# A LoRA and mixture-of-experts kernel on one core: the W stage opens with a quarter of all eight blocks, two sums to a PSUM bank, and six LoRA factors are issued behind it

## The chip, the cores and the metric

One core of one Trainium2 chip runs the whole kernel. The time is device microseconds of that core. The kernel before takes 283.78 us, the median of three runs (283.76 to 284.56). The names of the engines are those of the profile: PE is the matrix engine's products and PEld its weight loads, DVE is VectorE, ACT is ScalarE, POOL is GpSimd, SP is SyncE; SPq and ACTq are instructions that these two only issue, DMAs above all.

## The reference

```python
# x (8, 512, 2048); W (2048, 2048); b (2048); slot (8,) chooses LoRA factors for each batch
A, Bm = lora_As[slot], lora_Bs[slot]                      # (8, 2048, 16), (8, 16, 2048)
y = einsum('bti,oi->bto', x, W) + b + 2.0 * (x @ A) @ Bm  # conditioned layer
logits = einsum('bsd,ed->bse', y, route_w)                # 8 experts
weight = one_hot(argmax(logits)) * max(logits)
h = einsum('bsd,erd->bser', y, A_moe)                     # rank 16 of each expert
out = x + einsum('bser,eor->bso', weight[..., None] * h, Bw)
```

## The kernel before

y itself is never formed. Only 136 of its linear functions are used: the 128 rows of the experts' A and the 8 rows of route_w. They stand side by side as PT (2048 x 136). So the kernel first multiplies W with PT (the **W stage**), which gives a matrix M of 2048 x 136, and then multiplies x with M. All matrices are float32; M and x are split into a high and a low part (m_hi, m_lo, x_hi, x_lo), and three products of parts take the place of one.

**The W stage.** The inputs of W are cut into 8 blocks of 256 (`NWB`), its outputs into 4 quarters of 512 (`NWH`). A piece (block, part) is 512 KB, and 32 pieces go through a ring of 8 slots (`w_ring`). Four 128-row chunks times two halves of a block make 8 products of 136 columns, which the profile shows as 16 records. A block's two sums lie in the two banks of one PSUM tensor (`w_bank`), each in the first 136 of 512 columns, and are complete when all four parts were added. `ORDER` is the order of the pieces: all parts of blocks 0 to 3 (`OPEN` = 4) are taken part by part, and then blocks 4 to 7 each with its four parts. The first part of the opening is loaded in two halves (`load_open`, `w_open`): the head (W's first half piece and the PT rows that it needs, 392 KB) and half pieces of 256 KB. PT's other rows come behind the pieces that `PT_AFTER` names. SyncE issues all these loads, in order; from the ninth load on each waits until a piece is done (`t_w`).

After 20 pieces (`BP_AT`) the matrix engine computes the LoRA-B sums (L708, from `lb_cols`, which GpSimd rearranges) and the bias sum (L713). These go into `bank_l` and `bank_e[1]`, both in the tensor `bank_rl`.

**Taking the sums.** ScalarE copies a block's M out of PSUM: m_hi, and the 8 route columns into the two buffers of `ext` (`m_block`, L395). VectorE then forms m_lo = M - m_hi (`m_block`, L508) and counts it in `v_m`. The matrix engine waits for `v_m` where it begins a block whose PSUM tensor an earlier block used (`w_piece`). At `n == BP_AT // NWH`, 5, ScalarE takes the LoRA and bias sums (`bp`, `pb`), and issues eight DMAs from bp and one from pb into `g_a`, and then `load_a(2, NB)`: the A factors of batches 2 to 7, 128 KB each, into `la`. An engine's instructions and DMA issues are done in the order of its program.

**Behind the W stage.** For each batch `extension(b)` multiplies x with the 32 columns of `ext[b % 2]`: 8 route columns and the batch's 16 LoRA-A columns, which GpSimd copies there from `la` (`load_ext`, L367). The copy for batch 2 waits for all six factors of `load_a(2, NB)` (`d_la`). Then 8 steps of 6 products form h for the batch (L797, L811, L826). The order is: extension 0, steps of batch 0, extensions 1 and 2, steps of batch 1 with the output products of batch 0 between them, and so on. In the last step of batch 0, before the last product, the matrix engine waits for GpSimd's copy for batch 2:

```python
                        if b == 0 and j == NP2 - 1:
...
                                pe.wait_ge(g_ext, TWIN + 1)
```

ScalarE's `top(0)` (e_top, L455) follows extension 0. x comes in pieces of 1 MB through a ring of 12, issued by SyncE among and behind the last W loads; the outputs go back through the same ring.

## Time and profile before

| | us |
|---|---|
| median of three runs | 283.78 |
| span of the profiled execution, first to last instruction | 282.3 |
| PE busy | 276.7 |
| PEld busy | 220.0 |
| DVE busy | 200.5 |
| ACT busy | 110.2 |
| POOL busy | 15.0 |

The median lies 1.5 us over the profiled span; of the profiled execution the profile gives the span alone. The busy time is a share of the whole span and says which engine has no room. Where an engine waited, and for whom, stands in its timeline: the start of an instruction, its duration, and in brackets the idle time before it with the engine that ended it. Two views go by another clock: the landing of a DMA is counted from its issue, and the rows by slices of time are means.

### The profile page before, as it was taken

Reading aid. Unit: us, or ns where it says so; the run is one execution under the profiler, and the core shown is the slowest. Engines: PE = TensorE matmul, PEld = TensorE weight load, DVE = VectorE, ACT = ScalarE, POOL = GpSimd, SP = SyncE. Lnnn points to the kernel's source line nnn. Section 1 sums busy time; section 2 is a strip of 40 time slices with the busy share of each in tenths; the row PEclk is TensorE's granted clock in tenths of the full one; section 3 lists DMA queues with packets and bytes.
Section 4 is the critical chain, followed back from the end, with each engine's and each line's share of the span. In section 5 each row is a group of like instructions: output and inputs, shape, how many; then the busy total and the mean of one; then the engine's idle time right before and its main releaser. Section 6 shows DMA issues by size and latency. Waiting matters only on the chain.

```text
span 282.3 us, 4100 instructions
## 1 busy us (share of the span) xinstructions
PE 276.7 (98%) x1601; PEld 220.0 (78%) x1601; DVE 200.5 (71%) x223; ACT 110.2 (39%) x151; POOL 15.0 (5%) x46
## 2 busy tenths in 40 slices
PE   8999999999999999999999999999999999999993
PEld 5999999997773888888488758867885888588882
DVE  0053100077497889999889969996998799788794
ACT  0001201097684645534274346426533743370000
POOL 7600030000001000000000000000000000000000
PEclk9999999999999999999999999999999999999998
DMA  7999999999992034999966993999399859606688
GB/s 226 414 404 397 397 412 410 378 399 415 416 426 97 2 149 188 351 346 388 404 259 230 425 389 152 352 402 404 130 373 399 320 167 420 288 22 253 261 354 322
DMA packets 19014, 88.50 MB, mean 313 GB/s; under 512 B 2346, under 2 KB 4530, under 8 KB 11442
## 3 DMA queue, kind: packets, MB, share of 16 engines
q1 hardware_dynamic: 15696, 83.70, 75.7%
q10 hardware_dynamic: 3298, 4.54, 4.4%
q8 instruction: 12, 0.20, 0.3%
q14 instruction: 8, 0.07, 0.1%
HBM read 54.60 MB, written 33.55 MB: 312 GB/s over the span
## 4 chain that ended last, share of the span: by engine, by line
PE 90%; DVE 6%; DMA 2%; SPq 1%; issue 0%; DVEq 0%
PE bank_out L670 15%; PE bank_eh L797 11%; PE bank_eh L811 10%; PE bank_eh L826 10%; PE bank_out L736 9%; PE bank_out L759 9%; PE bank_out L750 9%; PE bank_rl L777 5%; PE bank_eh L777 5%; DVE x_ring L654 4%; PE bank_eh L670 2%; PE bank_rl L670 2%; DMA head_sb<-head 2%; PE bank_rl L708 1%; PE bank_eh L832 1%; PE bank_rl L831 1%
## 5 line engine op out<-in xcount | busy, mean ns | idle before, releaser
L393 ACT ACTIVATE x_hi<-x_ring 128x1024 fp32r<-128x1024 f32 x64 | 67.4, 1060 | 57.5 <-PE bank_eh L826 57.2
L506 DVE TENSOR_TENSOR x_lo<-x_ring,x_hi 128x1024 fp32r<-128x1024 f32 x64 | 77.5, 1220 | 8.6 <-ACT x_hi L393 8.6
L595 DVE TENSOR_TENSOR x_ring<-bank_out,x_ring 128x1024 f32<-128x1024 f32 x54 | 65.7, 1218 | 2.9 <-PE bank_out L759 2.8
L797 PE MATMUL bank_eh<-x_hi,m_hi 128*128 128x512 f32 x128 | 50.6, 395 | 0.0
L811 PE MATMUL bank_eh<-x_lo,m_hi 128*128 128x512 f32 x128 | 49.9, 390 | 0.0
L826 PE MATMUL bank_eh<-x_hi,m_lo 128*128 128x512 f32 x128 | 49.8, 389 | 0.0
L736 PE MATMUL bank_out<-wh_hi,bw_hi 128*128 128x512 f32 x120 | 46.7, 389 | 0.0
L750 PE MATMUL bank_out<-wh_lo,bw_hi 128*128 128x512 f32 x120 | 46.7, 389 | 0.0
L759 PE MATMUL bank_out<-wh_hi,bw_lo 128*128 128x512 f32 x120 | 46.7, 389 | 0.0
L670 PE MATMUL bank_out<-pt,w_ring 128*128 128x136 f32 x288 | 34.6, 279 | 0.0
L670 PEld LDWEIGHTS bank_out<-pt,w_ring 128*128 128x128 f32 x288 | 33.9, 190 | 0.2 <-DMA w_ring<-W 0.2
L797 PEld LDWEIGHTS bank_eh<-x_hi,m_hi 128*128 128x128 f32 x128 | 24.0, 188 | 10.7 <-issue 5.9
L826 PEld LDWEIGHTS bank_eh<-x_hi,m_lo 128*128 128x128 f32 x128 | 24.0, 188 | 5.1
L811 PEld LDWEIGHTS bank_eh<-x_lo,m_hi 128*128 128x128 f32 x128 | 24.0, 188 | 4.8
L759 PEld LDWEIGHTS bank_out<-wh_hi,bw_lo 128*128 128x128 f32 x120 | 22.5, 188 | 4.7
L750 PEld LDWEIGHTS bank_out<-wh_lo,bw_hi 128*128 128x128 f32 x120 | 22.5, 188 | 4.7
L736 PEld LDWEIGHTS bank_out<-wh_hi,bw_hi 128*128 128x128 f32 x120 | 22.5, 188 | 4.7
L777 PE MATMUL bank_rl<-x_ring,ext 128*32 128x512 f32 x128 | 14.6, 595 | 0.0
L777 PE MATMUL bank_eh<-x_ring,ext 128*32 128x512 f32 x128 | 14.5, 595 | 0.0
L393 ACT ACTIVATE wh_hi<-wh 128x512 fp32r<-128x512 f32 x8 | 5.1, 632 | 23.5 <-DVE wh L584 23.5
L506 DVE TENSOR_TENSOR m_lo<-bank_out,m_hi 128x256 fp32r<-128x256 f32 x6 | 2.5, 424 | 16.4 <-ACT ext L393 16.4
L506 DVE TENSOR_TENSOR bw_lo<-x_ring,bw_hi 128x2048 fp32r<-128x2048 f32 x1 | 2.3, 2291 | 14.5 <-ACT bw_hi L393 14.5
(99 smaller groups left out, 220.6 us busy)
## 6 DMA issues: line engine op xcount, KB each, us to landing
x_ring<-xT SPq DMA_DIRECT2D x32, 1024.0 KB, 8.0
outT<-x_ring SPq DMA_DIRECT2D x26, 1024.0 KB, 4.8
w_ring<-W SPq DMA_DIRECT2D x28, 512.0 KB, 10.8
outT<-x_ring SPq DMA_DIRECT2D x5, 512.0 KB, 2.8
outT<-x_ring ACTq DMA_DIRECT2D x4, 512.0 KB, 2.8
w_ring<-W SPq DMA_DIRECT2D x6, 256.0 KB, 5.3
outT<-x_ring SPq DMA_DIRECT2D x5, 256.0 KB, 2.7
x_ring<-loraB ACTq DMA_DIRECT2D x8, 128.0 KB, 9.8
```

The source lines that it names most:

```text
L393: act.activation(out, in_, ACT.Copy).then_inc(done, 1)
L506: dve.tensor_tensor(out, a, b, ALU.subtract).then_inc(done, 1)
L595: dve.tensor_tensor(x, out_bank(b, j)[:, :, :], x, ALU.add).then_inc(v_out, 1)
L654: dve.tensor_tensor(x, out_bank(NB - 1, c // 2)[:, c % 2, :], x, ALU.add).then_inc(v_out, 1)
L670: last = mm(bank, w_chunk(n, o, i), pt_chunk(k), start=(k == 0), stop=(k == C - 1))
L736: mm(out, bw_hi[:, o], hi, start=True, stop=False)
L750: mm(out, bw_hi[:, o], lo, start=False, stop=False)
L759: last = mm(out, bw_lo[:, o], hi, start=False, stop=True)
L777: last = mm(bank_e[b % 2][g * GROUP:(g + 1) * GROUP, :], ext[b % 2][:, c, :], x_pair(b, c // 2)[:, c % 2, :], start=(r == 0), stop=(r == C ...
L797: mm(bank_h, m_hi[:, c, :], hi, start=(c == 0), stop=False)
L811: mm(bank_h, m_hi[:, c, :], lo, start=False, stop=False)
L826: last = mm(bank_h, m_lo[:, c, :], hi, start=False, stop=(c == C - 1))
```

## The change

- `ORDER` begins with part 0 of all eight blocks, in two halves each; then come parts 1 to 3 of blocks 0 to 3, part by part, and then parts 1 to 3 of blocks 4, 5, 6 and 7. PT's later rows are issued behind loads 7, 10 and 13.
- Two blocks share a PSUM tensor: columns 0 to 135 of each bank for blocks 0 to 3, columns 136 to 271 for blocks 4 to 7 (block 4 with 2, 5 with 3, 6 with 0, 7 with 1). The LoRA-B sums and the bias sum take columns 272 to 407 of `bank_rl`, the tensor of blocks 3 and 5. Only the first product in a bank carries the start flag.
- The sums are taken in the order 0, 1, 3, 2, 4, 5, 6, 7 (`TAKEN`). The LoRA and bias sums, with their nine DMAs, are taken before block 3; block 2 is taken when block 4 is done.
- The matrix engine waits for `v_m` at one place of the W stage alone: part 1 of block 5, for the third m_lo.
- `load_a(2, NB)` stands behind the last block's copies.

```diff
--- before.py
+++ after.py
@@ -73,11 +73,16 @@
     HEAD_W = HO * WI
     PT_PARTS = [(4, 8), (8, 12), (12, 16)]
     NPT = len(PT_PARTS)
-    PT_AFTER = {3: 0, 6: 1, 9: 2}
+    PT_AFTER = {7: 0, 10: 1, 13: 2}
     OPEN = NWB // 2
-    ORDER = [(blk, part) for part in range(NWH) for blk in range(OPEN)] + [
-        (blk, part) for blk in range(OPEN, NWB) for part in range(NWH)]
+    ORDER = [(blk, 0) for blk in range(NWB)] + [
+        (blk, part) for part in range(1, NWH) for blk in range(OPEN)] + [
+        (blk, part) for blk in range(OPEN, NWB) for part in range(1, NWH)]
     DONE = [max(n for n in range(NWP) if ORDER[n][0] == blk) + 1 for blk in range(NWB)]
+
+
+    TAKEN = [0, 1, 3, 2, 4, 5, 6, 7]
+    READY = [DONE[OPEN] if blk == 2 else DONE[blk] for blk in range(NWB)]
     assert ER == P and WI == 2 * P and NWB == NP2 and NB * R == P and BIAS_ROW < GROUP
 
     ctx = ExitStack()
@@ -169,7 +174,7 @@
         d_slots, d_bias, d_bw, d_lb, d_la0, d_la = (sem(n) for n in ("d_slots", "d_bias", "d_bw", "d_lb", "d_la0", "d_la"))
         d_pt = [sem(f"d_pt{i}") for i in range(NPT)]
         d_head = [sem(f"d_head{h}") for h in range(NHEAD)]
-        d_w_half = [sem(f"d_w_half{n}") for n in range(1, OPEN)]
+        d_w_half = [sem(f"d_w_half{n}") for n in range(1, NWB)]
         d_w = [sem(f"d_w{i}") for i in range(WRING)]
         d_x = [sem(f"d_x{i}") for i in range(XRING)]
         d_out = [sem(f"d_out{i}") for i in range(XRING)]
@@ -232,7 +237,11 @@
 
         def w_bank(blk):
 
-            return (*bank_out, bank_eh, bank_rl)[blk] if blk < OPEN else bank_out[blk % 2]
+            bank = (*bank_out, bank_eh, bank_rl)[blk] if blk < OPEN else (bank_eh, bank_rl, *bank_out)[blk - OPEN]
+            at = PN * (blk // OPEN)
+            return bank[:, :, at:at + PN]
+
+        lora_sums, bias_sums = (bank_rl[:, i, 2 * PN:3 * PN] for i in (1, 0))
 
         def out_bank(b, j):
 
@@ -273,7 +282,7 @@
 
             def load_open(h):
                 sp.dma_start(head_sb[:, h, :], head[h]).then_inc(d_head[h], 16)
-                for n in range(1, OPEN):
+                for n in range(1, NWB):
                     blk, part = ORDER[n]
                     o = slice(h * HO, (h + 1) * HO)
                     sp.dma_start(w_ring[:, n, o, :], W[blk, part, :, o, :]).then_inc(d_w_half[n - 1] if h == 0 else d_w[n], 16)
@@ -294,8 +303,8 @@
 
             for h in range(NHEAD):
                 load_open(h)
-            for n in range(OPEN - 1, NWP):
-                if n >= OPEN:
+            for n in range(NWB - 1, NWP):
+                if n >= NWB:
                     load_w(n)
                 if n in PT_AFTER:
                     k = PT_AFTER[n]
@@ -394,8 +403,10 @@
 
             def m_block(n):
 
-                act.wait_ge(t_w, DONE[n])
-                sums = w_bank(n)[:, :, 0:PN]
+                act.wait_ge(t_w, READY[n])
+                if n == OPEN:
+                    act.wait_ge(v_m, OPEN)
+                sums = w_bank(n)
                 copy(m_hi[:, 2 * n:2 * n + 2, :], sums[:, :, E:PN], a_m)
                 for i in range(2):
                     copy(ext[i][:, 2 * n:2 * n + 2, 0:E], sums[:, :, 0:E], a_m)
@@ -410,26 +421,25 @@
                 copy(x_hi[:, g % SRING, :, :], x_pair(b, j), a_xhi)
 
             act.wait_ge(g_zero, ZEROED)
-            for n in range(NWB):
+            for n, blk in enumerate(TAKEN):
                 if n == 0:
                     act.wait_ge(t_w, LB_AT)
                     for b in range(NB):
                         act.dma_start(lb[:, b, :, :].rearrange("p c r -> p (c r)"),
                                       loraB[bass.ds(slot[b], 1), :, :].rearrange("s p n -> p (s n)")).then_inc(d_lb, 16)
                     load_a(0, 2)
-                if n == BP_AT // NWH:
+                if n == 2:
                     act.wait_ge(t_bp, 1)
-                    act.activation(bp[:, E:XN], bank_l[:, 0:PN], ACT.Copy, scale=float(SCALING)).then_inc(a_bp, 1)
-                    act.activation(bp[:, 0:E], bank_l[:, 0:E], ACT.Copy, scale=float(SCALING)).then_inc(a_bp, 1)
                     act.wait_ge(t_pb, 1)
-                    copy(pb[:, E:XN], bank_e[1][0:1, 0:PN], a_bp)
-                    copy(pb[:, 0:E], bank_e[1][0:1, 0:E], a_bp)
+                    act.activation(bp[:, E:XN], lora_sums, ACT.Copy, scale=float(SCALING)).then_inc(a_bp, 1)
+                    act.activation(bp[:, 0:E], lora_sums[:, 0:E], ACT.Copy, scale=float(SCALING)).then_inc(a_bp, 1)
+                    copy(pb[:, E:XN], bias_sums[0:1, :], a_bp)
+                    copy(pb[:, 0:E], bias_sums[0:1, 0:E], a_bp)
                     act.wait_ge(a_bp, 4)
                     act.wait_ge(g_const, 4)
                     for b in range(NB):
                         act.dma_start(g_a[E:E + R, b, :], bp[b * R:(b + 1) * R, :]).then_inc(d_g, 16)
                     act.dma_start(g_a[BIAS_ROW:BIAS_ROW + 1, :, :], pb[:, :].unsqueeze(1).broadcast_to([1, NB, XN])).then_inc(d_g, 16)
-                    load_a(2, NB)
                 if n == NWB - 2:
                     act.wait_ge(d_g, 16 * (NB + 1))
                     for part, form in G_PARTS:
@@ -446,7 +456,8 @@
                 if n == NWB - 1:
                     for j in range(SRING):
                         split_hi(0, j)
-                m_block(n)
+                m_block(blk)
+            load_a(2, NB)
 
             def top(b):
                 act.wait_ge(t_ext, b + 1)
@@ -506,7 +517,7 @@
                 dve.tensor_tensor(out, a, b, ALU.subtract).then_inc(done, 1)
 
             def m_block(n):
-                dve.wait_ge(a_m, 3 * (n + 1))
+                dve.wait_ge(a_m, 3 * (TAKEN.index(n) + 1))
                 sub(m_lo[:, 2 * n:2 * n + 2, :], w_bank(n)[:, :, E:PN], m_hi[:, 2 * n:2 * n + 2, :], v_m)
 
             def split_lo(b, j):
@@ -533,7 +544,7 @@
                     dve.wait_ge(v_pb, c)
                     dve.scalar_tensor_tensor(out=pb_sum[c % 2][:, :], in0=pt_chunk(c), scalar=bias_sb[:, c:c + 1],
                                              in1=pb_sum[(c - 1) % 2][:, :], op0=ALU.mult, op1=ALU.add).then_inc(v_pb, 1)
-            for n in range(NWB):
+            for n, blk in enumerate(TAKEN):
                 if n == NWB - 2:
                     for k, (part, form) in enumerate(G_PARTS):
                         dve.wait_ge(a_ghi, 2 * k + 1)
@@ -544,7 +555,7 @@
                 if n == NWB - 1:
                     for j in range(SRING - 1):
                         split_lo(0, j)
-                m_block(n)
+                m_block(blk)
 
             def sum_two(b):
                 dve.wait_ge(a_top, b + 1)
@@ -661,18 +672,20 @@
 
                 blk, part = ORDER[n]
                 for i in range(2):
-                    bank = w_bank(blk)[:, i, 0:PN]
+                    bank = w_bank(blk)[:, i, :]
                     for o in range(o0, o1):
                         k = part * WO + o
                         for p in range(NPT):
                             if blk == 0 and i == 0 and k == PT_PARTS[p][0]:
                                 pe.wait_ge(d_pt[p], 16)
-                        last = mm(bank, w_chunk(n, o, i), pt_chunk(k), start=(k == 0), stop=(k == C - 1))
+
+                        last = mm(bank, w_chunk(n, o, i), pt_chunk(k), start=(k == 0 and blk < OPEN), stop=(k == C - 1),
+                                  skip_group_check=True)
                 return last
 
             def w_open(h):
 
-                for n in range(OPEN):
+                for n in range(NWB):
                     if n == 0:
                         pe.wait_ge(d_head[h], 16)
                     elif h == 0:
@@ -686,8 +699,8 @@
             def w_piece(n):
 
                 blk, part = ORDER[n]
-                if part == 0 and blk >= OPEN:
-                    pe.wait_ge(v_m, blk - OPEN + 1 if blk < OPEN + 2 else blk - 1)
+                if part == 1 and blk == OPEN + 1:
+                    pe.wait_ge(v_m, 3)
                 pe.wait_ge(d_w[n % WRING], 16 * loads_in_slot(n))
                 w_rows(n, 0, WO).then_inc(t_w, 1)
 
@@ -697,20 +710,19 @@
                 mm(bank_h[:, :], warm[:, :], warm[:, :].unsqueeze(1).broadcast_to([P, T // P, P]), start=True, stop=True)
             for h in range(NHEAD):
                 w_open(h)
-            for n in range(OPEN, BP_AT):
+            for n in range(NWB, BP_AT):
                 w_piece(n)
 
             pe.wait_ge(g_lb, 1)
-            pe.wait_ge(v_m, OPEN)
             for c in range(C):
                 if c == C - 1:
                     pe.wait_ge(g_const, CONSTS)
-                last = mm(bank_l[:, 0:PN], lb_cols[:, c, :, :].rearrange("p b r -> p (b r)"), pt_chunk(c),
-                          start=(c == 0), stop=(c == C - 1))
+                last = mm(lora_sums, lb_cols[:, c, :, :].rearrange("p b r -> p (b r)"), pt_chunk(c),
+                          start=False, stop=(c == C - 1), skip_group_check=True)
             last.then_inc(t_bp, 1)
 
             pe.wait_ge(v_pb, C)
-            mm(bank_e[1][:, 0:PN], ones[:, :], pb_sum[(C - 1) % 2][:, :], start=True, stop=True).then_inc(t_pb, 1)
+            mm(bias_sums, ones[:, :], pb_sum[(C - 1) % 2][:, :], start=False, stop=True, skip_group_check=True).then_inc(t_pb, 1)
             for n in range(BP_AT, NWP):
                 w_piece(n)
 
@@ -769,7 +781,7 @@
                         if T * c % PIECE == 0:
                             x_landed(pe, NQ * b + T * c // PIECE)
                         if b == 0 and c % 2 == 0:
-                            pe.wait_ge(a_m, 3 * (c // 2 + 1))
+                            pe.wait_ge(a_m, 3 * (TAKEN.index(c // 2) + 1))
                         if c == C - 1 and b == 0:
                             pe.wait_ge(v_m, NWB)
                         if c == C - 1 and b > TWIN:
@@ -779,6 +791,7 @@
                 last.then_inc(t_ext, 1)
 
             pe.wait_ge(g_ext, 1)
+            pe.wait_ge(v_m, 5)
             for b in range(NB):
 
                 if b != TWIN:
```

**The matrix engine behind the bias sum.** `bank_eh` and `bank_rl` are the PSUM tensors, d_w0 to d_w7 the slots of the W ring. Before:

```order
L713 MATMUL bank_rl<-pb_sum,ones 128x136 [waits v_pb]
L670 MATMUL bank_out<-head_sb,w_ring 128x136 [waits d_w4,v_m]
L670 MATMUL bank_out<-head_sb,w_ring 128x136 x7
L670 MATMUL bank_out<-pt,w_ring 128x136 [waits d_w5]
L670 MATMUL bank_out<-pt,w_ring 128x136 x7
L670 MATMUL bank_out<-pt,w_ring 128x136 [waits d_w6]
L670 MATMUL bank_out<-pt,w_ring 128x136 x7
L670 MATMUL bank_out<-pt,w_ring 128x136 [waits d_w7]
```

And now:

```order
L725 MATMUL bank_rl<-pb_sum,ones 128x136 [waits v_pb]
L682 MATMUL bank_eh<-pt,w_ring 128x136 [waits d_w4]
L682 MATMUL bank_eh<-pt,w_ring 128x136 x7
L682 MATMUL bank_eh<-pt,w_ring 128x136 [waits d_w5]
L682 MATMUL bank_eh<-pt,w_ring 128x136 x7
L682 MATMUL bank_eh<-pt,w_ring 128x136 [waits d_w6]
L682 MATMUL bank_eh<-pt,w_ring 128x136 x7
L682 MATMUL bank_rl<-pt,w_ring 128x136 [waits d_w7,v_m]
L682 MATMUL bank_rl<-pt,w_ring 128x136 x7
```

Behind the bias sum stood block 5's four pieces; now block 4's three stand there, in `bank_eh`, and then block 5's first in `bank_rl`, which waits for v_m.

**ScalarE around the LoRA sums.** Before:

```order
L422 ACTIVATE bp<-bank_rl 128x136 [waits t_bp]
L423 ACTIVATE bp<-bank_rl 128x8
L393 ACTIVATE pb<-bank_rl 1x136 [waits t_pb]
L393 ACTIVATE pb<-bank_rl 1x8
L430 DMA g_a<-bp 16x144 [waits g_const,a_bp]
L430 DMA g_a<-bp 16x144 x7
L431 DMA g_a<-pb 1x8x144
L388 DMA la<-loraA 128x256 x6
L393 ACTIVATE bw_hi<-x_ring 128x2048 [waits d_bw]
L393 ACTIVATE m_hi<-bank_out 128x256 [waits t_w]
```

And now:

```order
L434 ACTIVATE bp<-bank_rl 128x136 [waits t_pb,t_bp]
L435 ACTIVATE bp<-bank_rl 128x8
L402 ACTIVATE pb<-bank_rl 1x136
L402 ACTIVATE pb<-bank_rl 1x8
L441 DMA g_a<-bp 16x144 [waits g_const,a_bp]
L441 DMA g_a<-bp 16x144 x7
L442 DMA g_a<-pb 1x8x144
L402 ACTIVATE m_hi<-bank_rl 128x256 [waits t_w]
L402 ACTIVATE ext<-bank_rl 128x2x8 x2
L402 ACTIVATE m_hi<-bank_eh 128x256 [waits t_w]
L402 ACTIVATE ext<-bank_eh 128x2x8 x2
L402 ACTIVATE m_hi<-bank_eh 128x256 [waits v_m,t_w]
```

Block 3 (`bank_rl`), block 2 and block 4 (`bank_eh` twice) are copied behind the nine DMAs into `g_a`, and the six loads of `la` have left this place; they stand between the copies of the last block and e_top.

## Rows read from the trace of the kernel before

**Rows 1.** The page: busy time; GB/s in 40 slices of 7.06 us.

```profile
PE 276.7 (98%) x1601; PEld 220.0 (78%) x1601; DVE 200.5 (71%) x223; ACT 110.2 (39%) x151; POOL 15.0 (5%) x46
...
GB/s 226 414 404 397 397 412 410 378 399 415 416 426 97 2 149 188 351 346 388 404 259 230 425 389 152 352 402 404 130 373 399 320 167 420 288 22 253 261 354 322
```

**Rows 2.** Weight loads of the opening: start us, us, what, [idle before].

```profile
3.83 0.99 PEld L670 LDWEIGHTS bank_out<-head_sb 128*128 128x128 f32 x8 [0.57 <-DMA head_sb<-head]
...
5.97 0.99 PEld L670 LDWEIGHTS bank_eh<-head_sb,w_ring 128*128 128x128 f32 x8 [0.22 <-DMA w_ring<-W]
...
8.42 0.99 PEld L670 LDWEIGHTS bank_out<-head_sb 128*128 128x128 f32 x8 [0.53 <-DMA head_sb<-head]
9.34 1.00 PEld L670 LDWEIGHTS bank_out<-head_sb,w_ring 128*128 128x128 f32 x8
...
12.36 3.77 PEld L670 LDWEIGHTS bank_out<-pt,w_ring 128*128 128x128 f32 x32 [0.17 <-DMA w_ring<-W]
```

**Rows 3.** Timeline of the matrix engine behind the bias sum.

```profile
46.06 2.02 PE L670 MATMUL bank_out<-head_sb,w_ring 128*128 128x136 f32 x16
...
60.89 2.02 PE L670 MATMUL bank_out<-head_sb,w_ring 128*128 128x136 f32 x16
...
68.39 1.92 PE L777 MATMUL bank_eh<-x_ring,ext 128*32 128x512 f32 x16
```

**Rows 4.** Timeline of ScalarE behind the LoRA sums.

```profile
46.03 0.28 ACT L422 ACTIVATE bp<-bank_rl 128x136 f32<-128x136 f32 x1 [3.17 <-PE bank_rl L708]
...
46.27 0.32 ACT L393 ACTIVATE pb<-bank_rl 1x136 f32<-1x136 f32 x2
46.62 5.10 ACTq L430 DMA_DIRECT2D g_a<-bp  x8
51.75 1.21 ACTq L431 DMA_DIRECT2D g_a<-pb  x1
53.06 2.76 ACTq L388 DMA_DIRECT2D la<-loraA  x6
55.87 1.91 ACT L393 ACTIVATE bw_hi<-x_ring 128x2048 fp32r<-128x2048 f32 x1 [9.28 <-issue]
```

**Rows 5.** Timeline of ScalarE, then VectorE, at the end of the W stage.

```profile
58.08 4.73 ACT L393 ACTIVATE g_st<-g_a 32x1024 fp32r<-32x1024 f32 x6
...
63.92 0.38 ACT L393 ACTIVATE m_hi<-bank_out 128x256 fp32r<-128x256 f32 x1
...
64.48 3.90 ACT L393 ACTIVATE x_hi<-x_ring 128x1024 fp32r<-128x1024 f32 x4
...
72.10 0.69 ACT L455 ACTIVATE e_top<-bank_eh,e_bias 64x512 f32<-64x512 f32 x1 [3.07 <-PE bank_eh L777]
...
64.48 0.42 DVE L506 TENSOR_TENSOR m_lo<-bank_out,m_hi 128x256 fp32r<-128x256 f32 x1 [1.59 <-ACT ext L393]
```

**Rows 6.** First and last of six later LoRA factors: issue, and to landing.

```profile
L388 ACTq DMA_DIRECT2D la<-loraA x1: 348/348/348, 53.1 to 53.1; - x1
...
DMA to landing us min/median/max: 6.4/6.4/6.4
...
L388 ACTq DMA_DIRECT2D la<-loraA x1: 393/393/393, 55.4 to 55.4; - x1
...
DMA to landing us min/median/max: 16.6/16.6/16.6
```

**Rows 7.** GpSimd's copy for batch 2; PE at the end of batch 0.

```profile
72.20 0.41 POOL L372 COPY ext<-la 128x256 f32<-128x256 f32 x1 [31.22 <-PE bank_eh L777]
...
83.26 0.39 PE L811 MATMUL bank_eh<-x_lo,m_hi 128*128 128x512 f32 x1
83.48 0.39 PE L826 MATMUL bank_eh<-x_hi,m_lo 128*128 128x512 f32 x1
```

**Rows 8.** The warm-up products, timeline of the matrix engine.

```profile
1.00 3.02 PE L697 MATMUL bank_eh<-warm 128*128 128x512 bf16 x7 [1.00 <-DVE warm L521]
```

**Rows 9.** One us near the end: busy us, granted clock, DMA share, GB/s.

```profile
280.00:281.00 1.00, 0.00 (x0) 0.00 (x0) 0.00 (x0) 0.00 (x0) 0.00 (x0) 0.61 0.97 373
```

## The prediction

> **What bounds the kernel now.** I read the page first. The matrix engine is busy for 276.7 us of a span of 282.3 us, 98% of it [rows 1]. Whatever lengthens or shortens that engine's unbroken stream moves the end by as much; nothing else does. The same rows show the DMA engines at 378 to 426 GB/s, about their best, from the second slice of 7.06 us to the twelfth, which ends at 84.7 us, so in the W stage and behind it the order of the transfers matters too. A difference under 0.3% of 283.78 us, 0.85 us, counts as no change.
>
> Second, the weight loads of the opening, where a late transfer shows as a gap between starts [rows 2]. A half block (8 records) takes 0.93 us when nothing is missing (8.42 to 9.34 us). The eight half blocks take 12.36 - 3.83 = 8.53 us where 8 x 0.93 = 7.44 would do: 1.1 us is lost. It lies at three places: 0.3 us before the block at 5.97 (3.83 + 2 x 0.93 = 5.69), 0.6 us before the second head at 8.42 (5.97 + 2 x 0.93 = 7.83), and 0.23 us before the first full piece at 12.36 (9.34 + 3 x 0.93 = 12.13).
>
> Third, the matrix engine's timeline of the middle [rows 3]: from 46.06 to 68.39 twelve pieces of 16 records run without a gap, 1.86 us each (14.83 us for the first eight, to 60.89).
>
> Fourth, ScalarE just behind the LoRA-B sums [rows 4]. It copies the sums, then issues eight small DMAs in 5.10 us, one in 1.21 us, and the six later LoRA factors in 2.76 us. From 46.62 to 55.82 it does nothing else. The copies of block 5, whose sums are ready at 46.06 + 4 x 1.86 = 53.5, come only behind bw_hi, after 57.7. That costs nothing before, because the matrix engine alternates between two PSUM tensors there and asks for those copies only at 60.89.
>
> **The change, part by part.**
>
> *Opening.* Eight half blocks come before the second head, and no PT rows or full piece is wanted until sixteen half blocks are done. The first three halves keep their place in the queue, so the 0.3 us before 5.97 stays. The fourth to seventh come where the second head came, which landed at about 8.4 us [rows 2]; each is two thirds of its size, and they are used 0.93 us apart while 262 KB arrives in 0.65 us at the 414 GB/s of the second slice [rows 1]. So the other 0.83 us goes: **-0.8 us** (bounds: nothing, if the fourth half comes as late as the head did, and -1.1 if all waiting goes). All that follows comes 0.8 us earlier. The W loads are wanted 0.8 us sooner while the DMA engines are full. I cost that at nothing: no piece waited for one [rows 3], and the six LoRA factors (0.79 MB, 1.9 us of full DMA engines at 414 GB/s) leave that stretch. If this cover were gone, it would cost at most the 0.8 us gained.
>
> *The sums go out in another order.* The new code lets blocks 4 and 5 share a bank with 2 and 3. Block 5's second piece (part 1) writes the tensor that holds block 3 and the two LoRA sums, so it waits until VectorE has taken block 3's m_lo (the third of v_m). ScalarE takes block 3 only behind the nine DMA issues. Before, no wait of the matrix engine stood so close behind these issues. The count, in the time of the old trace:
> - The copies of bp now also wait for the bias sum. They start where pb's did (46.27 instead of 46.03), so the issues begin 0.24 us later, and with the 0.8 us at 46.06.
> - Nine issues, 46.62 to 52.96 = 6.34 us, end at 52.4. From the start of m_hi to the end of m_lo it takes 63.92 to 64.90 = 0.98 us [rows 5]. With 0.1 us of handing over, v_m reaches 3 at 53.5.
> - The matrix engine comes to that piece three pieces after the bias sum: 46.06 - 0.8 + 3 x 1.86 = 50.8.
> **The new wait is 53.5 - 50.8 = 2.7 us.** Queued behind it are the rest of W and everything else. So the W stage ends 1.9 us later than before (70.3). Bounds: 1.2 us if the eight small issues ran at the 0.46 us of the la issues (saves 8 x 0.18), 3.3 us if the two copies of bp and the two of pb each take their full time one behind the other and the hand-over is slow.
>
> *What follows on ScalarE* is long but fits: block 5 ends at 53.5 + 5.6 = 59.1, its copies 0.65, the g_st, beats and ahead work 58.08 to 63.92 = 5.8, block 6's copies 0.6, four x_hi 3.9 [rows 5]: 70.1, just before block 7's sums are ready at 70.3. No wait there. The extension waits for block 7's copies only at its last chunks.
>
> *The six LoRA factors* are issued behind block 7's copies, at 71.0, and take 2.76 us until 73.8; e_top is wanted at 72.10 + 1.9 = 74.0 [rows 5]. So the issuing is covered, by 0.2 us. Their landing is not. In the code the last product of batch 0's last block (L826, i = 1, j = 7) waits for g_ext of batch 2, GpSimd's copy, and that waits for all six. Before, the last of them landed at 55.4 + 16.6 = 72.0 [rows 6], and the matrix engine reached the product at 83.48 [rows 7]: 11 us of cover. Now:
> - The first of six landed 6.4 us after its issue, at 59.5, the last 12.5 us later: 2.5 us each, though 128 KB alone is 0.3 us at 414 GB/s [rows 1, 6]. While large transfers are queued on the other queue, a factor takes that long.
> - From 71.1 that gives 77.5 for the first, then 80.0, 82.5, 85.0. The x transfers keep the engines full to 84.7 us, and the next slice's 97 GB/s x 7.06 us is 1.65 us of full rate: full until 86.4 [rows 1]. The bytes are the same in all, so the queues run dry at 86.4 again; the LoRA rows, last issued and slowest, are in its tail, and rows of 1 KB alone are no faster. I take 87.0.
> - GpSimd's copy is 0.41 us [rows 7] and 0.1 us hands over: 87.5 for a product that stood at 83.48. The shift is 4.0 us in all, of which 1.9 was there already: **a second wait of 2.1 us**.
> Bounds: nothing, if the last lands before 84.9; 7.1 us in all if the pace of 2.5 us held to the end (77.5 + 12.5 = 90.0).
> Once such a wait is there, the first does not matter: without it the matrix engine would only wait longer here.
>
> *Behind it* all x of batches 1 and 2 has landed, and the two extensions run as before. The rest keeps its distances. The chain ends 4.0 us later: span 286.3. The median of three runs is 1.5 us over the profiled span, so the time is 283.78 + 4.0 = **287.8 us**.
>
> **A rule of the skill.** The rows show 6.4 us from issue to landing for the first factor and 16.6 us for the last [rows 6]; with them the sum is 287.8. The Trainium skill, page "DMA: Bandwidth & Descriptors", section "Anatomy of one DMA", gives a fit of about 2.0 us and the bytes over 436 GB/s for one DMA. By that the last factor would land at about 76 and the sum would be 285.7. The trace does not agree with it here, and the page speaks of one transfer, not of one behind a full queue; the rows decide.
>
> **The rivals.**
> - *The factors land in time.* The x loads are ahead by 0.79 MB now, and the factors might be served at once: last issue at 73.4, 6.4 us to landing, 79.8 us, before 85.4. Then only the first wait is left: 283.78 + 1.9 = 285.7. Against it stands the pace [rows 6]. 18%. (The page's fit above is this case.)
> - *The clock falls in a wait.* The seven warm-up products of 512 columns take 3.02 us, 0.43 each [rows 8], against 0.22 for one of as many columns later [rows 7]: 1.2 GHz instead of 2.4. At the end, when the matrix engine has nothing left to do, the mean granted clock of the microsecond from 280 is 0.61 [rows 9]. How long it takes to fall, these rows bound by some 3 us, about the length of the waits. The price of one warm-up is 3.02 - 7 x 0.22 = 1.5 us; after the first wait it would be swallowed by the second, after the second it counts: 289.3. 14%. The Trainium skill, "TensorE: Matmul & The Clock Gate", Part 1, says that an idle stretch puts the array back to half its clock; the trace's end agrees.
> - *The pace never frees up*: 289.5 to 290.9. 6%.
> - *Faster.* If ScalarE's issues did not hold up its copies, the first wait would not exist; with the factors landing as in the first rival, only the opening's -0.8 us would be left: 283.0. The point that decides is whether m_lo of block 3 is there by 50.8; it would take issues of 0.4 us in place of 0.64 and 1.21. The 9.3 us without work before bw_hi, put down to "issue" [rows 4], speak against. 6%.
> - *No change*: the gain of the opening and a wait of about its size. 6%.
>
> **How the numbers follow.** The forecast with both waits has 50%, 287.8. The cases that are slower by over 0.3% add up to 50 + 18 + 14 + 6 = 88%. The range leaves out the two quick cases and the far end of the slow ones: from 285.2, which takes in the single wait with its lower bound, to 290.1.
>
> **What would show it.** Weight loads of the opening 0.93 us apart with one gap near 6 us; one idle stretch of 2.7 us on the matrix engine near 51 us, ended by VectorE's m_lo on bank_rl, with ScalarE issuing DMAs just before; a second of 2 us near 85 us, ended by GpSimd's copy into ext, itself released by a DMA of la. I am wrong if the W stage ends before 69 us, if the last la lands before 84.9, or if the extensions of batches 1 and 2 wait for x.

## The result, and the profile after

| | us | ratio to before |
|---|---|---|
| kernel before, 6 runs | 284.02 (283.76 to 284.56) | 1 |
| changed kernel, 6 runs | 291.24 (289.45 to 293.49) | 1.0241, 95% interval 1.0223 to 1.026 |
| profiled execution of the changed kernel | 289.71, span 287.9, mean granted clock 1.0 | |

The change makes the kernel 2.4% slower. The forecast of 287.8 us had the sign and both waits, but was 3.4 us too low, and the range ended at 290.1, below the median. The profile's page, which answers to [rows 1]: busy time, the chain of waits by engine, GB/s in slices of 7.2 us.

```profile
PE 277.3 (96%) x1601; PEld 220.6 (77%) x1601; DVE 201.2 (70%) x223; ACT 110.0 (38%) x151; POOL 14.8 (5%) x46
...
PE 84%; DVE 6%; DMA 5%; ACTq 3%; issue 0%; ACT 0%; POOL 0%; DVEq 0%
...
GB/s 246 387 395 400 399 409 413 381 414 421 414 395 23 2 91 200 208 357 373 387 407 140 376 395 277 234 422 379 150 361 406 380 142 389 294 58 220 268 355 324
```

The matrix engine's work grew by 0.6 us, the span by 5.6: the rest is waiting. The chain now runs over DMAs for 5% of the span (2% before) and over ScalarE's issuing for 3% (ACTq, none before). The matrix engine's timeline finds both waits:

```profile
45.75 5.72 PE L682 MATMUL bank_eh<-pt,w_ring 128*128 128x136 f32 x48
54.03 5.83 PE L682 MATMUL bank_rl<-pt,w_ring 128*128 128x136 f32 x48 [2.55 <-DVE m_lo L517]
59.69 11.28 PE L682 MATMUL bank_out<-pt,w_ring 128*128 128x136 f32 x96
70.90 3.64 PE L789 MATMUL bank_eh<-x_ring,ext 128*32 128x512 f32 x32
...
85.77 0.39 PE L824 MATMUL bank_eh<-x_lo,m_hi 128*128 128x512 f32 x1
88.92 0.50 PE L839 MATMUL bank_eh<-x_hi,m_lo 128*128 128x512 f32 x1 [2.76 <-POOL ext L381]
89.35 3.64 PE L789 MATMUL bank_rl<-x_ring,ext 128*32 128x512 f32 x32
```

Against [rows 3] extension 0 starts at 70.90 instead of 68.39, 2.5 us later. Against [rows 7] the product stands at 88.92 instead of 83.48, 5.4 us later. Behind it all distances are as before, and the span ends 5.6 us later. Measured from start to start, with 5.55 us for three pieces and 0.23 us for one product, the two waits are 54.03 - 45.75 - 5.55 = 2.7 us and 88.92 - 85.77 - 0.23 = 2.9 us; the brackets say a little less, since a modelled end of a product overlaps its successor. The engines that release them, ScalarE first, then VectorE:

```profile
46.01 0.28 ACT L434 ACTIVATE bp<-bank_rl 128x136 f32<-128x136 f32 x1 [7.17 <-PE bank_rl L725]
...
46.59 5.11 ACTq L441 DMA_DIRECT2D g_a<-bp  x8
51.73 1.21 ACTq L442 DMA_DIRECT2D g_a<-pb  x1
52.98 0.38 ACT L402 ACTIVATE m_hi<-bank_rl 128x256 fp32r<-128x256 f32 x1 [6.42 <-issue]
```

```profile
53.55 0.42 DVE L517 TENSOR_TENSOR m_lo<-bank_rl,m_hi 128x256 fp32r<-128x256 f32 x1 [14.25 <-ACT ext L402]
```

m_lo ends at 53.97 and the piece starts at 54.03. Then GpSimd's copy for batch 2, and the landing of the six factors (the first of them, then the last):

```profile
88.46 0.40 POOL L381 COPY ext<-la 128x256 f32<-128x256 f32 x1 [46.39 <-DMA la<-loraA]
```

```profile
L397 ACTq DMA_DIRECT2D la<-loraA x1: 348/348/348, 71.1 to 71.1; - x1
...
DMA to landing us min/median/max: 8.3/8.3/8.3
```

```profile
L397 ACTq DMA_DIRECT2D la<-loraA x1: 392/392/392, 73.5 to 73.5; - x1
...
DMA to landing us min/median/max: 14.9/14.9/14.9
```

The first factor landed at 71.1 + 8.3 = 79.4, the last at 73.5 + 14.9 = 88.4. The microseconds around it (busy PE, granted clock, DMA share, GB/s) show what it waited for: the end of the load queues.

```profile
84.00:85.00 1.00, 1.00 (x6) 1.00 1.00 401
85.00:86.00 1.00, 1.00 (x6) 1.00 0.95 358
86.00:87.00 1.00, 0.16 (x1) 1.00 0.50 184
87.00:88.00 1.00, 0.00 (x0) 1.00 0.19 67
88.00:89.00 1.00, 0.08 (x1) 1.00 0.00 0
```

Not all runs are like the profiled one. Two of the six (289.45 and 289.71 us) kept a granted clock of 1.0; the other four (291.2 to 293.49) had a mean clock of 0.985 to 0.994. The median of 291.24 lies among these, and the account above explains 289.7. The other 1.5 us were the open question at this point.

### The profile page after: what moved, and what is told of

Its sections match the earlier page's. It is cut to its first block, busy times and chain, and to the rows that moved or that the text cites. A ratio compares the mean times of both kernels' runs of the same rounds, so it can differ in the third digit from the quotient of the medians.

```text
span 287.9 us, 4103 instructions
## 1 busy us (share of the span) xinstructions
PE 277.3 (96%) x1601; PEld 220.6 (77%) x1601; DVE 201.2 (70%) x223; ACT 110.0 (38%) x151; POOL 14.8 (5%) x46
## 4 chain that ended last, share of the span: by engine, by line
PE 84%; DVE 6%; DMA 5%; ACTq 3%; issue 0%; ACT 0%; POOL 0%; DVEq 0%
PE bank_out L682 11%; PE bank_eh L810 9%; PE bank_eh L839 9%; PE bank_eh L824 9%; PE bank_out L748 9%; PE bank_out L771 9%; PE bank_out L762 9%; PE bank_rl L682 5%; DMA la<-loraA 5%; PE bank_rl L789 5%; PE bank_eh L789 4%; DVE x_ring L665 4%; PE bank_eh L682 3%; ACTq L441 2%; PE bank_rl L720 1%; PE bank_eh L710 1%
## 5 line engine op out<-in xcount | busy, mean ns | idle before, releaser
L682 PE MATMUL bank_out<-pt,w_ring 128*128 128x136 f32 x192 | 22.9, 279 | 0.0
L682 PEld LDWEIGHTS bank_out<-pt,w_ring 128*128 128x128 f32 x192 | 22.5, 190 | 0.0
L682 PE MATMUL bank_rl<-pt,w_ring 128*128 128x136 f32 x96 | 11.9, 280 | 2.6 <-DVE m_lo L517 2.6
L682 PEld LDWEIGHTS bank_rl<-pt,w_ring 128*128 128x128 f32 x96 | 11.4, 190 | 2.8 <-DVE m_lo L517 2.8
```

Of the source, the lines that this page charges most:

```text
L682: last = mm(bank, w_chunk(n, o, i), pt_chunk(k), start=(k == 0 and blk < OPEN), stop=(k == C - 1), skip_group_check=True)
```

## The experiments

Three theories had to be told apart: that each wait has the cause the prediction gave; that the factors' late landing comes from their place in the program alone; and that the time above 289.7 us comes from the clock falling in a wait. The kernel before has mean clocks of 0.996 to 1.0 in its runs beside these; below, a clock that "fell" is a mean of 0.994 or less. Where runs fall into two groups, each run's mean granted clock stands beside it.

### The factors issued early

```diff
                     load_a(0, 2)
+                    load_a(2, NB)
...
                 m_block(blk)
-            load_a(2, NB)
```

> The changed kernel with the six later LoRA factors issued at once behind the first two (ScalarE, before the first block's copies). Theory (two waits, the second set by the landing of the factors): the wait at the end of batch 0, 2.8 us in the changed kernel's trace, is gone; extension 1 begins some 15.4 us behind the start of extension 0, as before, so the profiled span falls from 287.9 to about 284.8 and the wait for m_lo near 51 us stays at 2.5 to 2.8 us. Time 286.5, some runs up to 1.5 us more if the clock falls in that wait. Rival (the wait is caused by something else, the extensions or GpSimd's order): the time stays at 289.5 to 291.

Measured: 288.18 us (286.23 to 288.35), ratio 1.0115 (1.0086 to 1.0144). The second wait is gone. The runs fall in two groups: 286.23 and 286.35 at clock 1.0, the other four, 288.08 to 288.35, at 0.993 or 0.994. The profiled one is of the second kind. The matrix engine, then windows (busy PE, clock, DMA share, GB/s):

```profile
54.28 7.22 PE L682 MATMUL bank_rl<-pt,w_ring 128*128 128x136 f32 x48 [2.56 <-DVE m_lo L517]
```

```profile
53.00:54.00 1.00, 0.00 (x0) 0.87 1.06 372
54.00:56.00 2.00, 1.72 (x7) 0.50 1.05 357
56.00:58.00 2.00, 2.00 (x15) 0.71 1.04 408
58.00:60.00 2.00, 2.00 (x20) 1.00 1.00 408
```

Near the end of a wait of 2.6 us the clock falls to 0.50, that is to 1.2 GHz, and returns between 56 and 58. The 48 records take 7.22 us where the changed kernel's profiled run took 5.83 behind the same wait. So the same program with the same wait keeps its clock in some runs and loses it in others, and the loss costs 2.0 us between the groups.

### Block 3's sums taken before the nine DMAs

```diff
                     copy(pb[:, 0:E], bias_sums[0:1, 0:E], a_bp)
+                    m_block(blk)
                     act.wait_ge(a_bp, 4)
...
-                m_block(blk)
+                if n != 2:
+                    m_block(blk)
             load_a(2, NB)
```

> The changed kernel with block 3's copies moved in front of the nine DMA issues; the factors stay behind the last block. Theory: m_lo of block 3 is ready near 47.5 us, long before the 51.4 us at which the matrix engine asks, so the first wait is gone and the W stage ends 2.7 us earlier, near 68.2. But the factors land when the x queue has run dry, at 87 to 88.5 whatever the matrix engine does, so the second wait grows to about 5 us and the time falls by no more than 1 us, to 288.5 to 290; a wait that long should let the clock fall in nearly every run and add 1.5 us. Rival (the two waits add up independently): 286.9 in clock-1.0 runs.

Measured: 292.29 us (291.44 to 293.25), ratio 1.0289 (1.0263 to 1.0314), so 1 us slower than the changed kernel, with one wait fewer, and above what was expected even with 1.5 us for the clock (290 to 291.5). The first wait is gone (extension 0 starts at 68.22), which shows that ScalarE's nine issues had made it. The factors are issued from 68.4 on, 2.7 us earlier, and the last still lands at 89.1:

```profile
89.10 0.40 POOL L381 COPY ext<-la 128x256 f32<-128x256 f32 x1 [47.08 <-DMA la<-loraA]
```

```profile
89.56 0.79 PE L841 MATMUL bank_eh<-x_hi,m_lo 128*128 128x512 f32 x1 [6.10 <-POOL ext L381]
90.28 5.03 PE L791 MATMUL bank_rl<-x_ring,ext 128*32 128x512 f32 x32
```

```profile
86.00:87.00 1.00, 0.00 (x0) 0.65 0.44 173
87.00:88.00 1.00, 0.00 (x0) 0.50 0.19 73
```

One wait of 6.1 us instead of two of under 3 lets the clock fall in every run (0.985 to 0.988). The product behind it takes 0.79 us instead of 0.50, the 32 records of the extension 5.03 instead of 3.64. From extension 1 to extension 3 this trace needs 53.5 us, the changed kernel's 52.1.

### Both edits

> Both edits. Theory: no wait left; only the opening's gain, between 0.2 us (as the changed kernel's trace showed) and 0.8 us (as predicted): 283.2 to 283.8, all runs with the clock at 1.0. Rival (sharing PSUM tensors or the new order costs something by itself): above 284.5.

Measured: 285.64 us (285.05 to 286.17), ratio 1.0046 (1.0029 to 1.0063), a miss. Both waits are gone, but others took their place:

```profile
54.71 3.97 PE L684 MATMUL bank_rl<-pt,w_ring 128*128 128x136 f32 x32 [0.91 <-DMA w_ring<-W]
...
62.78 7.68 PE L684 MATMUL bank_out<-pt,w_ring 128*128 128x136 f32 x64 [0.39 <-DMA w_ring<-W]
```

Extension 0 starts at 70.39 us, 2.2 us later than with the late factors (68.22), and the profiled span is 2.2 us over that of the next kernel but one (284.4 against 282.2), which has no wait. The factors are issued here from 22.8 us on and take 17 to 24 us to land, so 0.79 MB more go through the DMA engines ahead of the last pieces of W, which are barely on time. That costs about 2 us once nothing else makes W's pieces wait. It does not say that the place the factors had before, near 53 us, costs anything: with the old order of W, late factors were no faster than that (284.17 us, below).

### The kernel before, with the factors issued late

Only `load_a(2, NB)` is moved, behind the last block's copies.

> The kernel before, with only the issue of the six factors moved behind the last block's copies. Theory: issued near 69.1 us, the last lands at 86.5 to 88, and the product that waits for it, at 83.5 before, starts 4 to 5 us late: 288 to 289, plus up to 1.5 us where the clock falls. Rival (the factors land within 7 us of their issue when the queue is not held up by the changed order): 283.8 to 284.2.

Measured: 291.44 us (291.35 to 292.31), ratio 1.0257 (1.0239 to 1.0274). This one move alone loses what the whole change loses, and about 1 us more than was expected with the clock's share:

```profile
88.47 0.40 POOL L372 COPY ext<-la 128x256 f32<-128x256 f32 x1 [48.74 <-DMA la<-loraA]
```

```profile
88.92 0.79 PE L826 MATMUL bank_eh<-x_hi,m_lo 128*128 128x512 f32 x1 [5.60 <-POOL ext L372]
```

The last factor is issued 2.8 us earlier than in the changed kernel and lands at the same 88.4 us. What decides is when the queues drain, not the issue. The extension behind the wait took 5.92 us where it takes 3.64 at full clock. The clock again fell in every run (0.984 to 0.994).

### No wait: batch 2's factor on its own semaphore

On top of the second experiment:

```diff
                 if b == 2:
-                    pool.wait_ge(d_la, 16 * (NB - 2))
+                    pool.wait_ge(d_la2, 16)
+                if b == 3:
+                    pool.wait_ge(d_la, 16 * (NB - 3))
...
-                                      d_la0 if b < 2 else d_la, 16)
+                                      d_la0 if b < 2 else d_la2 if b == 2 else d_la, 16)
```

> The changed kernel with block 3's copies in front of the nine DMA issues, the factors still behind the last block, but batch 2's factor (issued first) on a semaphore of its own, so that GpSimd's copy for batch 2 waits for it alone. Theory: the first factor lands 8 us after its issue at 68.3, near 77, the product asks at about 83; both waits gone, and the W loads, which waited 1.3 us in the run with the factors early, run free. 283.5 to 284.2, clock 1.0 throughout. Rival (the new order of the pieces costs something by itself): above 285.

Measured: 283.75 us (283.1 to 285.12, 12 runs) against 284.31 of the kernel before beside it, ratio 0.9985 (0.9972 to 0.9999). It is the fastest median of all, though by less than the 0.3% that one comparison can tell. Both waits are gone, and W's pieces wait for no load. Batch 2's factor is there 12 us before the rest:

```profile
76.58 0.80 POOL L384 COPY ext<-la 128x256 f32<-128x256 f32 x1 [32.95 <-DMA la<-loraA]
88.88 0.40 POOL L384 COPY ext<-la 128x256 f32<-128x256 f32 x1 [11.49 <-DMA la<-loraA]
```

```profile
51.45 5.72 PE L687 MATMUL bank_rl<-pt,w_ring 128*128 128x136 f32 x48
...
68.22 3.64 PE L794 MATMUL bank_eh<-x_ring,ext 128*32 128x512 f32 x32
```

Extension 1 starts at 83.62, 15.4 us behind extension 0, as before.

### The changed kernel with the own semaphore alone

> The changed kernel with that semaphore alone. Theory: the second wait goes and the first stays: 286.3 in runs at clock 1.0 and 288.2 where the clock falls in the wait, as with the factors issued early. Rival (what delays the second place is the load on the DMA queues, not the count of six): a wait of 1 us or more stays at the product, and the time is above 287 at clock 1.0.

Measured: 286.57 us (286.17 to 288.42), ratio 1.009 (1.007 to 1.011). The four runs at clock 1.0 take 286.17 to 286.62, and the two at 0.993 and 0.994 take 288.42 and 287.9. The profiled run is one of the two. Its first wait and GpSimd's copy for batch 2, which now comes 7 us before the last landing:

```profile
54.36 7.25 PE L685 MATMUL bank_rl<-pt,w_ring 128*128 128x136 f32 x48 [2.55 <-DVE m_lo L520]
```

```profile
81.64 0.40 POOL L384 COPY ext<-la 128x256 f32<-128x256 f32 x1 [38.65 <-DMA la<-loraA]
```

So the count of six, not the load on the queues, made the second wait. What is left is the first wait, 2.6 us over the 283.75 of the kernel without waits at clock 1.0, plus 1.5 to 2 us when the clock falls.

### The kernel before, factors late, own semaphore

> The kernel before with the factors behind the last block and batch 2's factor on its own semaphore: the order of W is the old one. Theory: no wait, so the same as before within 0.3 us, 283.8 to 284.3; its difference to the changed kernel without both waits is then what the new order of W brings, 0 to -0.5 us. Rival (the gain of freeing the DMA queues during the W stage is what matters): under 283.5.

Measured: 284.17 us (283.62 to 284.53, 12 runs), ratio 1.000 (0.9991 to 1.0009). The late issue costs nothing once batch 2 need not wait for the other five. Against this kernel the one without waits has the new order of W and what belongs to it: the shared PSUM tensors, the order of taking the sums, and ScalarE's copies ahead of its issues. All that together is 284.17 - 283.75 = 0.4 us, half of what counts as a change here, so a gain of the new order is not shown.

### The matrix engine kept busy in both waits

Products whose results nobody reads stand in front of each wait, in the changed kernel:

```diff
                 if part == 1 and blk == OPEN + 1:
+                    pe.wait_ge(v_m, 2)
+                    for _ in range(13):
+                        mm(bank_out[0][:, 0, 3 * PN:T], ones[:, :], ones[:, 0:T - 3 * PN], start=False, stop=True,
+                           skip_group_check=True)
                     pe.wait_ge(v_m, 3)
...
+                                for _ in range(11):
+                                    mm(bank_out[0][:, 0, :], m_hi[:, c, :], hi, start=True, stop=True)
                                 pe.wait_ge(g_ext, TWIN + 1)
```

> The changed kernel, with products that nobody reads in front of its two waits: 13 of 104 columns in float32 (13 x 0.17 = 2.3 us of a 2.7 us wait) and 11 of 512 columns (11 x 0.227 = 2.5 us of a 3.2 us wait). Theory (the two kinds of runs of the changed kernel, 289.5 and 291.2 or more, differ by the clock falling in the waits): all runs near 289.5 at a granted clock of 1.0, so the median falls by 1.5 us although the engine has more to do. Rival (the two kinds come from the DMA side): the same spread, 289.5 to 293.5.

Measured: 291.31 us (290.41 to 292.47), ratio 1.0249 (1.0224 to 1.0274). The clock never fell (0.998 to 1.0), yet the median is no lower: a miss. Part of it is in the trace:

```profile
51.47 3.04 PE L705 MATMUL bank_out<-ones 128*128 128x104 f32 x26
```

The 13 added products took 2.9 us, not the 2.3 worked out, and ran past the end of the first wait (the piece starts at 54.35, not 54.03). Extension 1 starts 0.4 us later. The rest, 1.2 us, lies at the very end: from the last product to the end of the span it is 5.5 us here and 4.2 to 4.3 in the other eleven traces, so the last store is slower. That accounts for this one run. For the others it leaves the theory unproven: with the clock up, five runs took 290.4 to 292.5 us, no less than the changed kernel's with the clock fallen. So not all of the spread is the clock's, and this run does not show what a wait without the fall costs.

### Only the first wait, and filled

Twelve of the products before the first wait, on top of the own semaphore.

> The changed kernel with batch 2's factor on its own semaphore (so only the first wait is left), and 12 unread products of 104 columns (some 2.6 us) in front of that wait. Without them the runs fell into two kinds: 286.2 to 286.6 with the clock at 1.0 and 287.9 to 288.4 with a mean clock of 0.993. Theory (the clock falls in the idle 2.7 us and the pieces behind it run at half speed): with the array busy no run is of the second kind, all at 286.3 to 286.9. Rival (something else makes the second kind, the filling only costs): runs near 288.3 remain.

Measured: 286.87 us (286.03 to 288.18), ratio 1.0094 (1.0072 to 1.0116). All spans are 284.2 to 285.5 and all clocks at least 0.996, where without the filling two of six runs had fallen, with spans of 286.1 and 286.6.

```profile
52.00 2.82 PE L708 MATMUL bank_out<-ones 128*128 128x104 f32 x24
54.72 5.83 PE L685 MATMUL bank_rl<-pt,w_ring 128*128 128x136 f32 x48
```

The piece behind the wait takes 5.83 us, not 7.2. Two runs took 288 us all the same (287.99 and 288.18), which is the rival's sign. But their spans are 285.5 and 284.4: 2.5 and 3.8 us lie outside the span, where it is 1.8 or 1.9 in all other kernels' runs, and their clocks are 0.996 and 0.999. So this is not the second kind of run, though nothing here says what it is. Six runs against six are few. Taken together, the clock fell in none of the 11 runs with a filled wait, and in 15 of the 23 with a first wait left empty (the changed kernel's 11, the factors issued early and the own semaphore, 6 each). It fell in no run of the kernels without a wait either. So the idle time is what makes the clock fall. By the median the filling gains nothing.

### The changed kernel once more

> The changed kernel once more, for its spread beside the others on this chip. Theory: runs at clock 1.0 near 289.5; where the clock fell in the first wait the second absorbs it, so the time stays within 0.3 us of that; where it fell in the second, 291 to 293 with a mean clock of 0.985 to 0.994. Rival: times do not go with the granted clock.

Measured: 291.02 us (290.38 to 291.37, 5 runs), ratio 1.0241 (1.0227 to 1.0254). The clock fell in all five (0.991 to 0.994), and none is near 289.5, so the expectation that the second wait absorbs a fall in the first was missed. This time the profile caught it; the granted clock is back at 1.0 before the second wait:

```profile
54.55 7.42 PE L682 MATMUL bank_rl<-pt,w_ring 128*128 128x136 f32 x48 [2.55 <-DVE m_lo L517]
...
73.02 3.64 PE L789 MATMUL bank_eh<-x_ring,ext 128*32 128x512 f32 x32
...
90.19 0.49 PE L839 MATMUL bank_eh<-x_hi,m_lo 128*128 128x512 f32 x1 [1.92 <-POOL ext L381]
90.62 3.64 PE L789 MATMUL bank_rl<-x_ring,ext 128*32 128x512 f32 x32
```

Extension 0 is 2.1 us later than in the first profile (1.6 from the clock, 0.5 from a slower opening). The second wait shrinks by 0.85 us, and extension 1 is still 1.3 us later (90.62 against 89.35). Of these 1.3 us, 0.5 are a later last landing (GpSimd's copy starts at 88.97, not 88.46), and 0.8 a copy that took 1.17 us instead of 0.40. VectorE's timeline says why the copy was slow. First the first profile, then this one:

```profile
84.27 3.49 DVE L517 TENSOR_TENSOR x_lo<-x_ring,x_hi 128x1024 fp32r<-128x1024 f32 x3
```

```profile
86.39 3.49 DVE L517 TENSOR_TENSOR x_lo<-x_ring,x_hi 128x1024 fp32r<-128x1024 f32 x3
```

In the first profile the three x_lo end at 87.76, before the copy starts. Here VectorE is 2.1 us behind, as the matrix engine is. They end at 89.88, and the copy, begun beside them, ends at 90.14, 0.26 us behind them. The other traces agree. Of the 72 such copies behind 60 us in the twelve traces, seven more took 0.56 to 0.80 us. Each began while VectorE subtracted one SBUF tensor from another (x_lo or e_st), and each ended 0.25 to 0.27 us behind that. All others took 0.40 or 0.41. With the slower opening alone, 0.5 us, the x_lo would have ended near 88.3, ahead of the copy. So by this estimate the 0.8 us come from the clock after all, by way of VectorE. What delayed the landing stays open, and one trace doesn't tell what the other runs did.

## Why the prediction was wrong, step by step

**The first wait: right.** 2.7 us were forecast and 2.7 measured, with the cause as given. Both of its ends came 0.5 us later than forecast, because the opening brought less: m_lo at 53.97 instead of 53.5, and the piece was asked for at 51.3 instead of 50.8. The two kernels with the own semaphore, with and without this wait, measure its price end to end: 286.57 against 283.75 us; the four runs at clock 1.0 have 286.17 to 286.62.

**The opening's "-0.8 us": mis-sized.** The bias sum came 0.3 us earlier. Weight loads of the opening:

```profile
3.77 1.68 PEld L682 LDWEIGHTS bank_out<-head_sb 128*128 128x128 f32 x8 [0.52 <-DMA head_sb<-head]
...
7.42 0.99 PEld L682 LDWEIGHTS bank_rl<-head_sb,w_ring 128*128 128x128 f32 x8
...
12.05 1.00 PEld L682 LDWEIGHTS bank_out<-head_sb 128*128 128x128 f32 x8
```

The gaps before the second head and the first full piece did go: behind 7.42 the half blocks follow each other 0.93 us apart. But the first half block took 1.68 us instead of the 0.99 of [rows 2]. Its records have the duration of products at half clock, and the warm-up ahead of it took 3.17 us against 3.02 in [rows 8]. So here the clock rose some 0.7 us later relative to the work. This differs from trace to trace: ten of twelve have a slow first block of 1.2 to 2.1 us, with either order of W. This error did not reach the sum, since the second wait ends at a landing.

**The landing of the factors: the step that failed for the profiled execution.** The text said that "the queues run dry at 86.4 again" and that "I take 87.0". It was 88.4. In the trace of before, at 1 us resolution, the tail was there to read:

```profile
85.00:86.00 1.00, 1.00 (x16) 1.00 0.92 385
86.00:87.00 1.00, 1.00 (x16) 1.00 0.39 164
87.00:88.00 1.00, 1.00 (x15) 1.00 0.08 33
```

A mean over a slice of 7.06 us [rows 1], turned into microseconds at full rate, gives the end of the queues as if they stopped at full rate. They fade over two to three microseconds instead, and what is issued last and wanted whole lands at the end of that fade. 88.4 instead of 87.0 is the 1.4 us by which the product was later than forecast (5.4 for 4.0). Of the 289.71 - 283.78 = 5.9 us between the times, 0.5 are left. Some 0.2 of them lie behind the product. The rest is outside the span: the forecast took 1.5 us for it, and it is 1.8 or 1.9 in the runs of the changed kernel and of the kernel before that list both. The other assumption held: the pace of 2.5 us did free up. The factors landed at 79.4, 82.2, 85.1, 86.3, 86.8 and 88.4, 2.8 and 2.9 us apart while x was loading and 0.5 to 1.6 behind it. And no rule of a fixed cost per DMA holds here. The Trainium skill, "DMA: Bandwidth & Descriptors", "Anatomy of one DMA", gives about 2.0 us and the bytes over 436 GB/s for one that GpSimd issues. These are issued by ScalarE, behind a full queue, so the fit was not for them; the measured 8.3 us for the first and 14.9 for the last are far from it, as [rows 6] was. Here the last factor lands when the other queue's work ends.

**The clock: the term that the sum put at nothing, and the rest of the miss.** The median is 1.5 us over the profiled 289.71. The sum has nothing for the clock; the rival "the clock falls in a wait" got 14%. In nine of eleven runs of the changed kernel it fell (0.985 to 0.994), and these took 290.4 to 293.5 us, against 289.5 and 289.7 for the two at 1.0. Where the first wait stands alone, the price of 1.5 us was about right: 1.4 to 1.6 us on the 48 records, against 5.83, and 1.8 and 2.0 us between the groups of runs. Two parts of the reasoning were wrong. The first is the chance itself: since "these rows bound by some 3 us" how long the clock takes to fall, "about the length of the waits", the trace left it open (the last product ended at 278.06, and the clock fell between 280 and 281), and an open question deserved nearer to one in two than 14%. With the first wait alone, 2.6 us by the brackets, the clock fell in four of six runs of one kernel and in two of six of another. The second is that a fall in the first wait "would be swallowed by the second". In the one trace that shows it, the matrix engine's own lateness was: it came 2.1 us later to the product, and the landing, not this, ended the wait. But GpSimd's copy was taken to be 0.41 us whatever else runs, and it took 1.17 beside a VectorE that was late as well. So 0.8 us came back, and 0.5 more from a later landing.

How much of the median's 1.5 us is the clock's stays open. That the nine slower runs are the nine with the fallen clock speaks for it; that the runs with both waits filled kept the clock and took 290.4 to 292.5 us speaks against its being all. In which of the two waits the clock fell in the four slower runs beside the first profile no trace shows. The Trainium skill, "TensorE: Matmul & The Clock Gate", Part 1, says that an idle stretch puts the array back to half clock; the traces agree, down to the granted 0.50.

**"Once such a wait is there, the first does not matter": right for the product, wrong for the time.** Without the first wait the product stood at 89.56, with it at 88.92. But with one long wait, of 6.1 us here and 5.6 in the kernel before with late factors, the clock fell in all eleven runs, and nothing stands behind it to swallow the slow stretch.

**The rivals.** *The factors land in time* became true by another edit, the own semaphore: batch 2's factor landed at 81.6 us there. *Faster* needed ScalarE's copies before its issues; with both edits that is 283.75, where I had worked out 283.0. Most of the gap is the opening: it brought 0.2 us in that trace (extension 0 at 68.22 instead of 68.39), not 0.8.

**Two sums of the text.** The range's lower end, 285.2, is said to take in the single wait with its lower bound. That would be 283.78 + 1.2 - 0.8 = 284.2. And the upper bound of the shift is 90.0 + 0.5 - 83.48 = 7.0 us, not 7.1. Neither touches the miss, which is at the upper end.

## What to carry to other kernels

A transfer that the next step needs should have its own semaphore, or be counted apart from those issued behind it: here that was worth 4.7 us in the changed kernel, and it is what makes a late issue free. When a small transfer is issued behind large ones, take its landing from the fade of the queues in windows of 1 us, not from its bytes or from a mean over a slice. And price a new wait of the matrix engine of two to three microseconds at its length plus the chance of some 1.5 to 2 us of half clock behind it. A later wait swallows that for the matrix engine only: the other engines come late too, and what they then run beside can cost again. Put an engine's copies ahead of its DMA issues when another engine waits for them.

## What the hardware showed beyond expectation

- The last of the six factors landed between 88.4 and 89.1 us in seven kernels, and at 90.4 in the eighth, with the last issue anywhere from 70.5 to 75.6 us. In the eighth the queues ended later too: 104 GB/s from 88 to 89 us, where it was 0 in the changed kernel.
- The first factor took 8.1 to 8.7 us from issue to landing behind queued x loads, where it took 6.4 behind W loads [rows 6].
- At the program's start the PEclk figures of the page read full speed, while the seven warm-up products ran at 0.43 us each [rows 8], half speed. The start of a trace tells the clock by its durations only.
- GpSimd's copy of 128x256 took 0.40 us with VectorE idle beside it. The eight of 72 that took longer, up to 1.17 us, all began beside a VectorE subtraction of two SBUF tensors and ended 0.25 to 0.27 us behind it. Where the copy came first, by 0.01 to 0.02 us, the subtraction took longer: 0.92 or 0.93 us instead of 0.68.
- Times of a program on one core can differ outside the span: it is 1.8 or 1.9 us in the runs of all kernels but one, and in that one 2.5 and 3.8 us in the two runs that took 288 us.
